# Row moments shared between router and norm, head squares on ScalarE, one norm weight folded, maxima negated, scatters in threes

## The reference, cut to what matters

```python
xn = _layernorm(x, axis=-1)
x = x + _L0_attn_ref(xn, ...) + _L0_ffn_ref(xn, ...)   # 8 experts, 4 chosen per token
# inside _L0_attn_ref: 16 heads of 16
def _rms_norm(x, w):
    ms = jnp.mean(jnp.square(x), axis=-1, keepdims=True)
    return x * jax.lax.rsqrt(ms + EPS) * w
q_c_norm = _rms_norm(q_c, q_norm_w)
q = jnp.concatenate([q_c_norm, q_c_norm @ W_QR.T], -1)
k = jnp.concatenate([_rms_norm(k_c, k_norm_w), xh @ W_KR.T], -1)
attn = jax.nn.softmax(q @ k.T * HD ** (-0.5) + causal, axis=-1)
```

## Time and profile before

| what | value |
|---|---|
| median of 3 runs | 3066.34 us (3065.47 to 3067.68) |
| the profiled execution | 3062.34 us, its span 3060.4 us |
| busy: PE, DVE, ACT, POOL | 90%, 70%, 53%, 47% of the span |
| DMA | 580 MB, mean 190 GB/s |

### The profile page before, as it was taken

How to read it: one execution, slowest core, us unless ns; L and a number is a source line. 1 busy time by engine, 2 the same in 40 slices (tenths; PEclk the granted TensorE clock), 3 DMA queues, 4 the chain that set the end, 5 groups by cost and what they waited for, 6 DMA issues and landing times. The chain is left out here.

```text
span 3060.4 us, 61227 instructions
## 1 busy us (share of the span) xinstructions
PE 2769.5 (90%) x20990; PEld 2259.8 (74%) x20990; DVE 2129.6 (70%) x6019; ACT 1627.7 (53%) x3420; POOL 1437.1 (47%) x2201
## 2 busy tenths in 40 slices
PE   5878799999999999979999999999799999999995
PEld 3655588898889889756666666666688888888864
DVE  5788788788778778767788888866544445444565
ACT  3555444544544444556656656665455555555563
POOL 4475843443453444365556665332333323333487
PEclk8888899999999999999999999999999999999998
DMA  3566678888789788422434443210566666566445
GB/s 84 203 233 241 219 278 296 293 296 309 280 290 325 276 296 309 153 45 54 100 99 108 110 111 105 95 70 26 210 228 208 211 204 238 204 215 208 138 89 127
DMA packets 212006, 580.12 MB, mean 190 GB/s; under 512 B 24616, under 2 KB 146416, under 8 KB 167408
## 3 DMA queue, kind: packets, MB, share of 16 engines
q1 hardware_dynamic: 172528, 523.82, 48.8%
q0 software_dynamic: 36864, 51.14, 8.2%
q10 hardware_dynamic: 2304, 1.21, 0.1%
HBM read 450.14 MB, written 125.96 MB: 188 GB/s over the span
## 5 line engine op out<-in xcount | busy, mean ns | idle before, releaser
L494 PE MATMUL bank<-xh,gu 128*128 128x256 f32 x3520 | 672.5, 291 | 34.2 <-DVE gc L1683 26.1
L1154 POOL TENSOR_TENSOR al<-t,ah 128x512 fp32r<-128x512 f32 x220 | 283.2, 1287 | 875.5 <-ACT ah L1388 875.5
L494 PEld LDWEIGHTS bank<-xh,gu 128*128 128x128 f32 x3520 | 512.4, 190 | 58.5 <-issue 55.6
L1885 DVE TENSOR_REDUCE st<-bank 128x1 f32<-128x512 f32 (+3 forms) x1024 | 421.9, 481 | 152.8 <-PE bank L555 146.5
L537 PE MATMUL bank<-masks_bf,ident_bf 128*128 128x128 bf16 x1896 | 428.2, 249 | 101.8 <-DVE st L1885 38.0
L1485 ACT ACTIVATE pt<-bank 128x512 f32<-128x512 f32 (+1 forms) x1152 | 509.4, 543 | 19.0 <-PE bank L558 17.5
L555 PE MATMUL bank<-ksT,qsT 128*128 128x512 f32 (+3 forms) x1536 | 408.7, 368 | 5.7 <-DVE top L1883 2.9
L537 PEld LDWEIGHTS bank<-masks_bf,ident_bf 128*128 128x128 bf16 x1896 | 168.7, 98 | 303.5 <-DVE st L1885 96.4
L1493 ACT ACTIVATE oT<-bank 128x512 f32<-128x512 f32 x192 | 114.5, 596 | 503.0 <-PE bank L634 499.7
L558 PE MATMUL bank<-qaT,ksT 128*128 128x512 f32 (+3 forms) x1536 | 381.9, 364 | 0.0
L1388 ACT ACTIVATE ah<-t 128x512 fp32r<-128x512 f32 x220 | 138.9, 631 | 399.6 <-DVE t L1709 358.5
(11 more groups left out here) (257 smaller groups left out, 5137.7 us busy)
## 6 DMA issues: line engine op xcount, KB each, us to landing
gu<-wu_scratch SPq DMA_DIRECT2D x110, 1032.0 KB, 5.1
gu<-wu_scratch SPq DMA_DIRECT2D x110, 1024.0 KB, 7.4
dn<-wd_scratch SPq DMA_DIRECT2D x110, 1024.0 KB, 6.7
xs<-xs_scratch SPq DMA_DIRECT2D x110, 264.0 KB, 4.3
ys_scratch<-yb SPq DMA_DIRECT2D x110, 256.0 KB, 7.0
raw<-in_gu SPq DMA_DIRECT2D x16, 1024.0 KB, 5.7
wu_scratch<-hi SPq DMA_DIRECT2D x16, 1024.0 KB, 5.2
wu_scratch<-lo SPq DMA_DIRECT2D x16, 1024.0 KB, 10.7
```

What stands on the lines that cost most here:

```text
L494: mm = pe.matmul(bank[:, TS * h:TS * (h + 1)], gu[:, col:col + P], x[s % 2][:, TS * k:TS * (k + 1)], start=(n == 0), stop=(n == len(terms) ...
L1154: pool.tensor_tensor(em["al"][s % 2][:, m, :], em["t"][g % 2][:, :], em["ah"][s % 2][:, m, :].bitcast(F32), ALU.subtract).then_inc(al_read ...
L1885: ins = dve.reduce_max(st[:, 0, r:r + 1], bank[:, first:first + width], AX.X)
```

## The change

Five edits:

1. A tile `norms` with 20 columns for each of the 8 batches holds what router and latent norm need. `row_stats`, `row_std` and `normalize` use it for latent batches; for batches 1 to 7 `row_stats` and `row_std` are no longer called, and `normalize` waits for the router's power in their place. For batch 0 the router's moments and power are no longer taken, and it uses those of `row_stats(0)`.
2. For batches 1 to 7 ACT squares queries and keys right out of PSUM, two instructions of 2 x 128 columns per block, between its copies L1442 and L1444; the first waits until DVE has summed the former block (`hs_used`). DVE's product is left for batch 0 only.
3. The queries' norm weight and the 0.25 are folded: at the start `qkw[1]` and `four[:, 2]` are multiplied by `0.25 * qkw[0]`, and `norm_heads` weighs the keys only.
4. The reduction L1885 writes the negated maximum to the column that `shift` reads, and the negation L1901 is gone for latent and grouped batches.
5. In a pair with more than three scatters POOL waits, before the 4th, 7th and 10th, until PE has finished the next pair's query scores, the first half of this pair's key scores, and the second half.

```diff
+    norms = sb("norms", [P, B, 20])
...
+        def moments(n):
+            return norms[:, loc(n), :] if kinds[n] == "mla" else stats[n % 2]
+        def stats_of(n):
+            return sum(m == 0 or kinds[m] != "mla" for m in range(n + 1))
...
# POOL
-                    small = stats[n % 2]
-                    pool.wait_ge(var_ready, n + 1)
+                    small = moments(n)
+                    pool.wait_ge(var_ready, stats_of(n))
...
+                def paced(G):
+                    return ("q", G + 1, NU - 1), ("k", G, NU // 2 - 1), ("k", G, NU - 1)
...
-                    route_std(0)
                     route_std(1)
...
-                    if nxt and p == 0:
+                    if nxt and p == 0 and kinds[n + 1] != "mla":
                         row_std(n + 1)
...
-                    for b, t, k in scatter_at.get(G, ()):
+                    for i, (b, t, k) in enumerate(scatter_at.get(G, ())):
+                        if i % 3 == 0 and i:
+                            pool.wait_ge(s_full, S.full(paced(G)[i // 3 - 1]))
                         route_scatter(b, t, k)
...
# ACT, take_projected, after the copy L1442 and before L1444
+                            if n:
+                                if c == 0:
+                                    act.wait_ge(hs_used, NT * (n - 1) + t)
+                                act.activation(mems["mla"]["sq"][:, :].rearrange("p (m o) -> p m o", m=2)[:, :, P * c:P * (c + 1)],
+                                               a[:, 0:2 * P].rearrange("p (m o) -> p m o", m=2), ACT.Square).then_inc(hs_full, 1)
...
# ACT, route_rows
+                    if b == 0:
+                        act.wait_ge(acc_in[0], 16)
...
# DVE, normalize
-                    dve.wait_ge(std_ready, n + 1)
+                    if n and kinds[n] == "mla":
+                        dve.wait_ge(rows_in, 16 * rows_at[n])
+                        dve.wait_ge(r_std, n)
+                    else:
+                        dve.wait_ge(std_ready, stats_of(n))
...
# DVE, head_squares
+                    if n == 0:
+                        ... as before
+                    else:
+                        dve.wait_ge(hs_full, 2 * (NT * (n - 1) + t + 1))
+                        dve.tensor_reduce(own, flat[:, 0:2 * D].rearrange("p (h o) -> p h o", o=HD), AX.X,
+                                          ALU.add).then_inc(hs_used, 1)
+                        dve.wait_ge(hs_used, NT * (n - 1) + t + 1)
...
# DVE, norm_heads
-                    for m in range(2):
-                        w = bcast(bcast(mem["qkw"][:, m, :], 1, NT), 2, heads.stop - heads.start)
-                        dve.tensor_tensor(v[m], v[m], w, ALU.mult).then_inc(dve_step, 1)
+                    w = bcast(bcast(mem["qkw"][:, 1, :], 1, NT), 2, heads.stop - heads.start)
+                    chain(dve.tensor_tensor(v[1], v[1], w, ALU.mult))
...
# DVE, maxima and shift
-                                ins = dve.reduce_max(st[:, 0, r:r + 1], bank[:, first:first + width], AX.X)
+                                ins = dve.reduce_max(st[:, 1, r:r + 1], bank[:, first:first + width], AX.X, negate=True)
...
-                    if not spm:
-                        chain(dve.tensor_scalar(st[:, 1, :], st[:, 0, :], -1.0, None, ALU.mult))
-                    else:
+                    if spm:
...
# DVE, before pair 0
+                    qkw = mems["mla"]["qkw"]
+                    chain(dve.tensor_scalar(qkw[:, 0, :], qkw[:, 0, :], 0.25, None, ALU.mult))
+                    chain(dve.tensor_tensor(qkw[:, 1, :], qkw[:, 1, :], qkw[:, 0, :], ALU.mult))
                     dve.wait_ge(four_ready, 1)
+                    chain(dve.tensor_tensor(four[:, 2, :], four[:, 2, :], qkw[:, 0, :], ALU.mult))
...
-                    chain(dve.tensor_scalar(mems["mla"]["qkw"][:, 0, :], mems["mla"]["qkw"][:, 0, :], 0.25, None, ALU.mult))
...
-                    route_stats(0)
                     route_stats(1)
```

More of the change, by code:

```diff
@@ L385, in pipeline @@
         if "mla" in start:
+            hs_full, hs_used = new("hs_full"), new("hs_used")
             mla_ready, qk_ms, qk_std, qk_first, mla_out = (
@@ L1287, in route_std @@
                 def route_std(b):
-                    small = ro["stats"][b % 2]
-                    pool.wait_ge(r_var, b + 1)
+                    small = norms[:, b, :]
+                    pool.wait_ge(r_var, b)
                     pool.tensor_tensor(small[:, 4:8], small[:, 0:4], minus_half[:, 0:NT], ALU.pow).then_inc(r_std, 1)
@@ L1742, in row_stats @@
                 def row_stats(n):
-                    small = stats[n % 2]
+                    scratch, small = stats[n % 2], moments(n)
                     if kinds[n] == "gqa":
@@ L1752, in row_stats @@
                     for t in range(NT):
-                        dve.bn_stats(small[:, 40 + 6 * t:46 + 6 * t], src[t]).then_inc(dve_step, 1)
+                        dve.bn_stats(scratch[:, 40 + 6 * t:46 + 6 * t], src[t]).then_inc(dve_step, 1)
                     chain.n += NT
@@ L1756, in row_stats @@
                     for t in range(NT):
[L1757 removed]
+                        dve.bn_aggr(small[:, 8 + 2 * t:10 + 2 * t], scratch[:, 40 + 6 * t:46 + 6 * t]).then_inc(dve_step, 1)
                     chain.n += NT
@@ L2070, in route_means @@
                 def route_means(b):
-                    small = ro["stats"][b % 2]
+                    small = norms[:, b, :]
                     mean_var = small[:, 8:16].rearrange("p (t two) -> p t two", two=2)
-                    dve.wait_ge(r_std, b + 1)
+                    if b:
+                        dve.wait_ge(r_std, b)
+                    else:
+                        dve.wait_ge(std_ready, 1)
                     dve.scalar_tensor_tensor(small[:, 16:20], mean_var[:, :, 0], -1.0, small[:, 4:8],
@@ L2172, in pair_with_experts @@
                         pick_weight(FIRST_TILE[begins.index(G)])
-                    if n + 1 < nb and p == 0:
+                    if n + 1 < nb and p == 0 and kinds[n + 1] != "mla":
                         row_stats(n + 1)
@@ L2198, in pair_alone @@
                     n, p = divmod(G, NP)
-                    if n + 1 < nb and p == 0 and not grouped_at(n):
+                    if n + 1 < nb and p == 0 and not grouped_at(n) and kinds[n + 1] != "mla":
                         row_stats(n + 1)
```

16 lines of the change are left out of this document (7 added, 9 removed).

## The result

The changed kernel takes 3030.55 us (median of 4 runs, 3021.94 to 3040.37), before took 3065.90 in the same comparison; the ratio is 0.9898, 95% interval 0.9880 to 0.9916. Two later sets of runs of the same two kernels gave 0.9884 (0.9867 to 0.9901) and 0.9860 (0.9845 to 0.9875). By these three ratios the change is worth 31, 36 and 43 us (26 to 48 with the intervals), where 30.5 were forecast. The first and the third interval don't overlap: an interval holds for its own set of runs, and between sets the same pair of kernels moved by 0.4%. The profiled execution took 3030.08 us, its span 3028.5, 31.9 less than before.

A forecast was written before the change was run, and what follows sets the result against it. PE's work is unchanged, so only its idle time, mostly waits for DVE, can shrink: 16.7 + 1.9 + 6.0 + 0.5 + 5.4 = 30.5 us off, predicted 3036 from the median; own range 3024 to 3048, final range 3018 to 3056.

The forecast's parts named there:

- pair 0: Start and pair 0: one GpSimd power and half of the weights leave the path, 1.9 us off.
- router's pairs 1 to 20: Router's stage: less DVE work before PE's waits, minus added ACT squares and passed scatter waits, 6.0 us off.
- pairs 21 to 49: Expert stage: PE's waits for DVE's gate shrink, net 4.75 us a batch, 16.7 us off, bounds 10 to 22.
- pairs 50 to 63: Light pairs: squares add 2.3 us, waits behind the heads' roots and weights lose 2.8, so 0.5 us off.
- grouped stage: Pairs 64 to 127: only the negation goes, 27 PE waits by 0.2, 5.4 us off, bounds 1.6 to 10.
- half the weights: Expert batches: one of two weight operations goes, 0.65 us in pair 1 and part of 0.85 later.
- ScalarE's squares: ACT's added squares cost PE 0.3 us a pair, 1.2 an expert batch; full 0.77 in pairs 50 to 52.
- the failed step: Router's even pairs: next raw weights don't come earlier, limiting the gain to 0.5 us each in pairs 2, 4, 10, 12.
- The clock rival: Router's stage: shorter PE waits lift three odd pairs' clock, 11 us more, 3025, or as much the other way; chance 0.12.
- ACT takes DVE's place: Expert stage: squares delay tanh and high half, PE's waits pass to ACT, 3048; chance 0.21 together with the pacing rival.
- The pacing: Router pairs 15 to 17: scatter waits hold POOL, stack late, 9 us lost, 3045; chance 0.21 shared with ACT's rival.
- The table switches: ACT: each square brings a table switch, 28 x 2 loads, 72 us less the 30.5, 3108; chance 0.01.

The follow-up runs named there:

- set 3: Third set of follow-up runs, sharing its runs of before; in it the changed kernel, without edit, took 3020.12 us, ratio 0.9860.
- both cures: Changed kernel with ScalarE squaring only blocks 0, 2 of batches 1 to 6, and raw weights' high half split behind exponentials in router pairs 3 to 15: 3010.35 us.

## Why the prediction was right, and where not

The whole was right (3036 for 3030.55; 30.5 us off for 31.9 between the two profiles), partly by luck, because two errors cancel:

| term | forecast | between the profiles |
|---|---|---|
| pair 0 | 1.9 | 1.2 |
| router's pairs 1 to 20 | 6.0 | -2.7 (-2.6 and 4.2 in the two later profiles) |
| pairs 21 to 49 | 16.7 | 23.5 |
| pairs 50 to 63 | 0.5 | 2.8 (0.0 and 2.5 in the two later profiles) |
| grouped stage | 5.4 | 5.6 |
| the rest | 0 | 1.5 |

- **Expert stage, pair by pair.** Mechanism right, size 0.7 of what came. Pair 0 gave 2.0 (1.75 forecast), pairs 2 and 4 1.3 and 1.4 (1.35 each). The product's worth is shown by the edit undone: 1.36 and 1.35. More came off than the 0.68 us that the product takes in pair 10, without experts. The Trainium skill (GPSIMD Engine Reference, the table of engine properties) has GpSimd share its SBUF interfaces with VectorE, with contention by VectorE instructions that have two SBUF inputs; the trace agrees, though no run here took GpSimd's work away. Undersized were half the weights (1.9 a batch by its undoing; I had 0.65 and a part of 0.85), as pairs 6 and 7 alone have 0.34 and 0.72 of it, and the negation (0.8). The four undone edits add up to 6.6 a batch, the change gave 6.4: these terms were additive. The start gave 1.2 for 1.9: the power and the weights cost 0.7 each where they were put back, not 1.0 and 0.9.
- **ScalarE's squares.** 0.8 a batch for the 1.2 forecast. In pairs 50 to 52 they cost 0.3 each, not 0.77: PE's wait for the keys behind them rose from 1.01 to 1.28 us. With 0.8 for 2.3 there, and the roots' waits at 2.9 less (11.0 to 8.1; 2.8 forecast), the light pairs came better. In the second profile of the changed kernel it was lost again: pairs 54 and 55 took 13.1 and 14.0 us in place of 11.7 and 12.9, though PE's waits were the same within 0.3 us.
- **Router's stage: the failed step.** The 101 of 133 us at 0.81 that the prediction gives for this stage are pairs 0 to 7 alone; the whole of it is 262.9 of 332.1 at 0.84. I wrote of the raw weights that they "don't come earlier", and used it only as a limit on what even pairs could win. They did win, 1.0, 1.1, 1.0 and 0.6 in pairs 2, 4, 10 and 12 against 0.5 each. But the same sentence says that in the next pair they come later. Pairs 3, 5, 9, 11 and 13 then grew by 0.9, 1.5, 1.0, 5.7 and 2.9, where I had +0.3 for three of them and -1.1 for 5 and 13. For 3, 5, 11 and 13 the late split is shown by the runs that take it away; pair 9 was 1.3 and 2.0 us shorter than before in the two later profiles, and its growth in the first has no shown cause. Two others moved by more than their terms: pair 15 took 3.6 us less and pair 17 2.2 more, both unexplained. The clock rival had the right sign only in its last words ("or fall the other way by as much"): it happened in pairs 5, 11 and 13 of every profile of the changed kernel.
- **Grouped stage.** 27 waits by 0.2 gave what they should; the negation undone cost more, 7.5 to 8.6. VectorE isn't late alone in this stage, as the prediction has it: PE also waited 7.2 and 2.8 us for ScalarE's copies, before and after.
- **The rivals.** "ACT takes DVE's place" is refuted: gate waits are 1.6 us with none over 0.4 (under 10 and 1.2 were forecast). The pacing didn't hold POOL, and PE's waits for its stack fell from 17.9 to 15.0 us. The table switches didn't come either: 56 Squares between Exp and Tanh brought no load. The Trainium skill (ScalarE: Activation LUTs, "Table sets: the hidden batching unit") has functions come in sets and lists Tanh in the one with Exp. It doesn't say there which sets hold Square, so the switches of the rival were an assumption of mine, not what the page makes of this kernel.

## What to carry to other kernels

When a stage gets shorter but a transfer in it doesn't, the transfer's consumer moves later within the stage: look up what is queued behind that consumer, and put it in front. A shortening counts only to the next arrival. Here this is shown in router pairs 3, 5, 11 and 13. And read small edits in the stretch that repeats to a tenth of a us, not in the whole.

## What was not expected of the hardware

- In the first profile of the changed kernel and in that of set 3 a wait of PE of 1.2 to 2.4 us in the middle of router pairs 3, 5, 11 and 13 had 8 to 14 us at 1.2 GHz behind it, in the second one waits of up to 3.5 us as well. In pair 11 PE's busy time rose by 3.4 us (16.36 to 19.79) on top of 1.9 us more of waiting; without the wait (both cures) 3.4 us in the second half of the pair ran at that level. Before, a wait of 0.77 in pair 3 was already followed by some 10 us of it, one of 0.44 in pair 11 wasn't. The length of the wait alone doesn't decide: see the 1.46 us in pair 13 with the moments taken twice.
- The kernel before took 3062.7, 3095.7 and 3062.0 us in the three later sets of runs. What made the second slower isn't known; in its profiles three router pairs took 27 to 30 us where they take 20 to 24 in the others.
- A second pair of Squares of 0.38 us in the same place cost PE more than the first pair, 0.5 against 0.2 a block.
